# Message sums of a graph network: fp32 products with one-hot matrices widened by ScalarE, in place of three bf16 products with pieces split off by VectorE

## The reference, cut to what matters

```python
def _gnn_layer(nf, traj, src, dst, We, be, Wn, bn):
    ef = jnp.concatenate([nf[src], nf[dst], traj[:, None]], axis=-1)
    msg = jax.nn.leaky_relu(ef @ We.T + be, negative_slope=0.01)
    red = jax.ops.segment_sum(msg, dst, num_segments=nf.shape[0])
    h = jnp.concatenate([nf, red], axis=-1)
    return jax.nn.leaky_relu(h @ Wn.T + bn, negative_slope=0.01)
```

## Time and profile before

| what | value |
|---|---|
| median of runs | 13957.37 us |
| profiled execution | 13966.42 us, span 13965.2 us |
| VectorE (DVE) busy | 10842.4 us, 78% |
| TensorE (PE) busy | 9172.6 us, 66% |
| ScalarE (ACT) busy | 5627.0 us, 40% |
| GpSimd (POOL) busy | 4548.9 us, 33% |
| target phases of the layers | about 7061 to 8575, 9693 to 11210 and 12326 to 13850 us |
| target phase of the first stage | about 4590 to 5955 us |

### The profile page before, as it was taken

One profiled execution on the slowest core, in us unless ns is written; L12 is line 12 of the kernel. 1 busy time (PEld: TensorE's weight loads), 2 busy tenths in 40 slices (PEclk: granted clock), 3 DMA queues, 4 the chain that ended last, 5 costly groups with the idle time before them and its releaser, 6 DMA issues. The chain is left out here.

```text
span 13965.2 us, 514377 instructions
## 1 busy us (share of the span) xinstructions
PE 9172.6 (66%) x172644; PEld 7604.8 (54%) x172644; DVE 10842.4 (78%) x26542; ACT 5627.0 (40%) x15578; POOL 4548.9 (33%) x4413
## 2 busy tenths in 40 slices
PE   6777777762777666667766556666555566666566
PEld 4555555541666555556655554555555555555554
DVE  8999999964777899854479996445999854479997
ACT  4666666630333688743322222333222233322222
POOL 0000000047000677610056663001666600046664
PEclk9999999965555788768899998999999989999997
DMA  1000000011788666746655555666555646665555
GB/s 34 5 5 6 5 5 6 3 25 30 238 241 241 181 197 196 172 129 207 207 180 172 172 171 98 201 201 195 171 171 171 161 123 201 201 188 171 172 172 111
DMA packets 1700459, 1931.56 MB, mean 138 GB/s; under 512 B 222450, under 2 KB 1571268, under 8 KB 1699460
## 3 DMA queue, kind: packets, MB, share of 16 engines
q1 hardware_dynamic: 977585, 893.89, 22.1%
q0 software_dynamic: 199680, 520.06, 15.1%
q10 hardware_dynamic: 522544, 510.34, 10.4%
HBM read 1202.74 MB, written 725.45 MB: 138 GB/s over the span
## 5 line engine op out<-in xcount | busy, mean ns | idle before, releaser
L1563 POOL DMA_INDIRECT work<-rows,quad_at x2928 | 3091.0, 1056 | 4501.8 <-DMA rows<-work 2007.4
L1378 DVE COPY work<-bank 128x256 f32<-128x256 f32 (+1 forms) x3840 | 1630.7, 425 | 1773.0 <-PE bank L1355 1748.6
L1408 PE MATMUL bank<-work 128*128 128x64 bf16 x46848 | 2077.6, 199 | 1361.4 <-DVE hr L1655 1352.2
L1355 PE MATMUL bank<-work 128*128 128x64 bf16 x46080 | 2726.2, 211 | 0.0
L1408 PEld LDWEIGHTS bank<-work 128*128 128x128 fp8e4 (+1 forms) x46848 | 1848.9, 102 | 1517.7 <-issue 1464.9
L1329 ACT COPY work<-tabs 128x192 bf16 x3840 | 1348.9, 351 | 2819.9 <-PE bank L1355 1579.4
L1588 ACT COPY work<-tabs 128x192 bf16 x2928 | 1028.9, 351 | 3548.4 <-PE bank L1604 3242.2
L1355 PEld LDWEIGHTS bank<-work 128*128 128x128 fp8e4 x46080 | 2394.1, 109 | 0.0
L1350 PE MATMUL bank<-wtraj,side 128*128 128x64 bf16 x11520 | 1772.3, 205 | 925.1 <-ACT work L1329 657.8
L521 ACT ACTIVATE work<-work,tabs 128x128 bf16<-128x128 bf16 x6250 | 1919.2, 427 | 935.0 <-DVE work L721 935.0
L1350 PEld LDWEIGHTS bank<-wtraj,side 128*128 128x128 bf16 x11520 | 1194.0, 104 | 1237.4 <-DVE work L1378 580.1
(11 more groups left out here) (323 smaller groups left out, 12309.8 us busy)
## 6 DMA issues: line engine op xcount, KB each, us to landing
work<-hits_g SPq DMA_DIRECT2D x1464, 256.0 KB, 2.7
rows<-work ACTq DMA_DIRECT2D x1440, 256.0 KB, 2.1
work<-hits_s SPq DMA_DIRECT2D x1440, 128.0 KB
hits_g<-work SPq DMA_DIRECT2D x976, 128.0 KB
rows<-work ACTq DMA_DIRECT2D x480, 260.0 KB, 4.6
work<-rows,quad_at POOLq DMA_INDIRECT x3904
work<-meta_src SPq DMA_DIRECT2D x480, 128.0 KB
hits_s<-work SPq DMA_DIRECT2D x480, 128.0 KB, 4.2
```

The source lines that it names most:

```text
L1355: last = ten.matmul(home, hits[n][:, q % GROUP_LOT, slots], window[q % 4][:, k * D:(k + 1) * D], start=False, stop=k == 2, skip_group_chec ...
L1378: vec.tensor_copy(made[n][:, q % GROUP_LOT, :], bank[q % 4][:, 0:QUAD * width]).then_inc(s_read, 1)
L1408: last = ten.matmul(to[:, 0:D], hits_of(j), piece_of(j), start=j == 0 and k == 0, stop=j == QUAD - 1 and k == 2, skip_group_check=True)
L1563: pool.indirect_dma_start(quads[g // 2 % (GATHERED // 2)][:, half(g)], None, table, bass.IndirectOffsetOnAxis(ap=quad_at[:, g:g + 1], axis ...
```

## The change: what it does

In `target_phase`, `less` and `split` go. The message stays one fp32 tile. ScalarE gets a new step, `as_float`: it widens the straight half of a group's one-hots from fp8 to fp32 (128 x 512) into one of four tiles `hits_f`. `scatter` then makes four fp32 products per group in place of twelve bf16 ones. VectorE's order becomes add(p), keep, keep, leaky(p). The semaphores `s_rest` and `s_split` go, and `s_hits` comes. `first_target_phase` now writes the straight one-hots in plain slot order, so its ScalarE cast reads with a stride of two elements; before, the read and the write both ran straight and the two slots of a couple lay interleaved.

```diff
@@ first_target_phase
-                sca.copy(hits_home[q % 4].bitcast(FP8)[:, SLOTS:2 * SLOTS], hits_b[q % 4].rearrange("p j c i -> p (j c i)"),
-                         saturate=False)
+                to = hits_home[q % 4].bitcast(FP8)[:, SLOTS:2 * SLOTS].rearrange("p (j i c) -> p j i c", i=2, c=P)
+                sca.copy(to, hits_b[q % 4].rearrange("p j c i -> p j i c"), saturate=False)
@@ target_phase, tiles
-        msg, rest = ([room.cut(2 * QUAD * D) for _ in range(4)] for _ in range(2))
-        low = [room.cut(QUAD * D, BF16) for _ in range(4)]
+        msg = [room.cut(2 * QUAD * D) for _ in range(4)]
+        hits_f = [room.cut(SLOTS) for _ in range(4)]
@@ scalar
+            def as_float(g, q, lap):
+                sca.wait_ge(s_in[q // 2], since_in + 16 * (lap + 1))
+                at_least(sca, s_sum, g - 3, since)
+                settle(sca, "scalar", g)
+                sca.copy(hits_f[q % 4], hits_home[q // 2][:, q % 2, :].bitcast(FP8)[:, SLOTS:2 * SLOTS]).then_inc(s_hits, 1)
...
                 sca.copy(window[q % 4].unsqueeze(1), tabs[:, 1, bass.ds(w, 1), :]).then_inc(s_window, 1)
+                if not isinstance(g, int) or g >= 2:
+                    as_float(g - 2, (q - 2) % LAP, lap - (q < 2))
@@ tensor, scatter
-                    ten.wait_ge(s_split, since_pairs + lap * (LAP // 2) + (q // 2 + 1))
+                    ten.wait_ge(s_leaky, since_pairs + lap * (LAP // 2) + (q // 2 + 1))
+                ten.wait_ge(s_hits, since + g + 1)
                 at_least(ten, s_kept, g - 3, since)
-                settle(ten, "tensor", g)
...
-                scatter_pieces(ten, sums[q % 4], lambda j: in_twos[:, j // 2, :, j % 2],
-                               [each(upper(msg[q // 2])), each(upper(rest[q // 2])), each(low[q // 2])]).then_inc(s_sum, 1)
+                rows = msg[q // 2][:, half(q)]
+                for j in range(QUAD):
+                    last = ten.matmul(sums[q % 4][:, 0:D], hits_f[q % 4][:, j * P:(j + 1) * P], rows[:, j * D:(j + 1) * D],
+                                      start=j == 0, stop=j == QUAD - 1)
+                last.then_inc(s_sum, 1)
@@ vector
-            def less(p):
...
-            def split(p):
...
-                if 1 <= p <= pairs:
-                    less(p - 1)
-                if p < pairs:
-                    leaky(p)
-                if 1 <= p <= pairs:
-                    split(p - 1)
                 if p >= 3:
                     keep(2 * p - 6)
                     keep(2 * p - 5)
+                if p < pairs:
+                    leaky(p)
```

More of the change, by code:

```diff
@@ L1538, in target_phase @@
         s_in = [sem_of(f"sums_in{n}", True) for n in range(4)]
-        s_window, s_before, s_added, s_leaky, s_rest, s_split, s_sum, s_kept = (sem_of("sums_" + what, True) for what in (
-            "window", "before", "added", "leaky", "rest", "split", "sum", "kept"))
+        s_window, s_before, s_added, s_leaky, s_hits, s_sum, s_kept = (sem_of("sums_" + what, True) for what in (
+            "window", "before", "added", "leaky", "hits", "sum", "kept"))
         past = number - 1
@@ L1588, in step @@
                 sca.copy(window[q % 4].unsqueeze(1), tabs[:, 1, bass.ds(w, 1), :]).then_inc(s_window, 1)
+                if not isinstance(g, int) or g >= 2:
+                    as_float(g - 2, (q - 2) % LAP, lap - (q < 2))
             laps(sca, NG, step)
+            for g in (NG - 2, NG - 1):
+                as_float(g, g % LAP, g // LAP)
         @block.tensor
@@ L1609, in scatter @@
                 if q % 2 == 0:
-                    ten.wait_ge(s_split, since_pairs + lap * (LAP // 2) + (q // 2 + 1))
+                    ten.wait_ge(s_leaky, since_pairs + lap * (LAP // 2) + (q // 2 + 1))
+                ten.wait_ge(s_hits, since + g + 1)
                 at_least(ten, s_kept, g - 3, since)
-                settle(ten, "tensor", g)
-                hits = hits_home[q // 2][:, q % 2, :].bitcast(FP8)
-                each = lambda ap: lambda j: ap[:, half(q)][:, j * D:(j + 1) * D]
-                in_twos = hits[:, SLOTS:2 * SLOTS].rearrange("p (j c i) -> p j c i", c=P, i=2)
-                scatter_pieces(ten, sums[q % 4], lambda j: in_twos[:, j // 2, :, j % 2],
-                               [each(upper(msg[q // 2])), each(upper(rest[q // 2])), each(low[q // 2])]).then_inc(s_sum, 1)
+                rows = msg[q // 2][:, half(q)]
[3 more added lines that the diff above has]
+                last.then_inc(s_sum, 1)
             def step(g, q, lap):
@@ L1640, in leaky @@
                 vec.scalar_tensor_tensor(msg[p % 4], msg[p % 4], SLOPE, msg[p % 4], ALU.mult, ALU.max).then_inc(s_leaky, 1)
-            def less(p):
-                vec.wait_ge(s_leaky, since_pairs + p + 1)
-                vec.tensor_tensor(rest[p % 4], msg[p % 4], upper(msg[p % 4]), ALU.subtract).then_inc(s_rest, 1)
-            def split(p):
-                vec.wait_ge(s_rest, since_pairs + p + 1)
-                vec.tensor_tensor(low[p % 4], rest[p % 4], upper(rest[p % 4]), ALU.subtract).then_inc(s_split, 1)
             def keep(g):
```

## The result

The change makes the kernel slower by more than a tenth. Its executions took 15560.31 to 16355.92 us, against 13954.09 to 13963.7 before; the ratio is 1.1155, with a 95% interval of 1.1133 to 1.1177. Later executions took 16351.26 (e1) and 16346.46 to 16349.05 us (e14, a ratio of 1.172 [1.1686, 1.1754]).

A forecast was written before the change was run, and what follows sets the result against it. VectorE was taken to bound the middle at 3.057 us a pair, then the one-hot load loop at 2.93. 13966 - 164 (middle) + 47 (phase ends) + 15 (low clock) = 13864, less 9 for the runs' median: 13855 us; range 13600 to 14060.

The forecast's parts named there:

- What bounds the kernel before: Target phases: VectorE paces the middle at 3.06 us a pair; the one-hot load loop paces the end, 3.68 measured.
- ScalarE, first stage, VectorE: VectorE falls to 1.85 us a pair, ScalarE needs at most 2.24; first stage's strided cast costs nothing.
- The window copies queued behind the casts: ScalarE copy needed by a pair's second before_message, queued behind as_float's wait: costed at nothing, a few tenths per pair if uncovered.
- The fp32 record: Scatter on TensorE: the weight load sets the pace, 0.111 us a record at 2.4 GHz, 0.22 at 1.2 GHz.
- Rival 3: Scatter's load and product don't overlap: 0.164 us a record, 3.32 a pair, 14380 us total; chance 0.08.
- The loop of load, before_message and scatter: Target phase middle: scatter frees the one-hot load; 5.80 us for two pairs, 2.93 a pair with added waits, 164 us less.
- At the end of a phase: Last 37 pairs of each target phase: 4.1 us a pair taken, 47 us more over three phases.
- GpSimd's floor: Target phase gathers, 1.055 us each with 0.30 between: at least 2.71 us a pair.
- Rival 2: One-hot load in the middle lands later: at 3.0 us, 3.08 a pair, about 14050 us total; chance 0.14.
- Low clock in the middle: Target phases about 2% of the time at 1.2 GHz, about 4.9 us a pair there; 15 us more taken.
- Theory A1: Forecast of e2: array's idle time behind loads keeps the clock low; doubled columns give 2.4 GHz, 13750 to 14050 us.

The follow-up runs named there:

- e1: The changed kernel run again with no edit: 16351.26 us.
- e14: The changed kernel once more, on a chip of the usual pace: 16346.46 and 16349.05 us.
- e4: Changed kernel with twelve bf16 products per group and VectorE's split back, ScalarE's casts kept: 13990.43 us beside 13953.33 for the kernel before.
- e3: Changed kernel with 160 bf16 products of 384 columns ahead of each layer's target phase, as a warm start: 15717.12 us.
- e6: Kernel of e2, with the one-hot load waiting for before_message and as_float of pair p-4, not its scatter: 13455.34 us, ratio 0.9642 to the kernel before.
- e2: Changed kernel with 128 moving columns instead of 64 in each fp32 product of scatter: 13885.18 us.
- e13: Kernel of e2 with 96 moving columns in place of 128, on a chip of the usual pace: 13896.0 us.
- e8: Changed kernel with 64 in place of 128 stationary columns in each fp32 product, leaving out sums of each window's upper half: 13454.46 us.
- e7: Changed kernel, 64 moving columns kept, with one unread bf16 product of 384 columns ahead of each scatter: 14068.04 us.

## Why the prediction was wrong

**What bounds the kernel before: right.** In the middle it is VectorE. e4 puts VectorE's two operations back and has the old pace, which agrees.

**ScalarE, first stage, VectorE: right, but for one wait.** The cast takes 0.618 us (0.62 was taken), and the cast with the strided read lasts 0.619 us (median) as before. VectorE was to be busy near 0.6 of the time; at 2.4 GHz it was, 601.39 of 1088 us (e3), and 35% at 1.2 GHz. The window copies queued behind the casts, which I had costed at nothing, held TensorE for 33.8 us in 118 of the 368 pairs of that stretch, 0.09 us a pair; with the loop opened (e6) these waits are gone.

**The fp32 record: right at both levels.** 0.111 was predicted at 2.4 GHz and 0.112 measured (e2); 0.22 at 1.2 GHz, and 0.213 measured. That the load sets it is shown by the moving columns, 64 (e3), 96 (e13) or 128 (e2) at the same 0.112, and that it goes with the stationary columns by e8. Rival 3 (load and product one after another) falls with them. The way to 0.22 held some luck: the earlier trace rows show no clock level, and the profile has a granted clock of 1.00 from 30 to 31 us, around that product, so "at the low clock level" was read into them because 0.22 is twice 0.111. In rival 3, half of 0.111 is 0.056 and not 0.053, which moves nothing that was forecast.

**The loop of load, before_message and scatter: right in its pace.** 2.93 us a pair was predicted for the middle at 2.4 GHz. 2.96 is measured with 64 columns (e3) and 2.99 with 128 (e2). TensorE's waits for loads came in 124 of e3's 368 pairs and not all through the phase, 69.8 us, so with the window copies 0.28 us a pair where 0.3 to 0.6 were expected. At the end of a phase 4.1 was taken, 3.85 measured. e6 opens the loop and lands on GpSimd's floor, for which I had 2.71; it is 2.64, since a gather there takes 1.02 instead of 1.055. Rival 2 (a later landing) would have shown as over 3.0 a pair in e2 and e3, and fell; a landing time at 2.4 GHz stands in no view of theirs.

**The clock: wrong, and it decides.** The step that failed is "Low clock in the middle": a pair "would need [...] about 4.9 us" at 1.2 GHz (its sum, 1.3 + 16 x 0.22, gives 4.82, and 4.74 was measured, so the price was near), but for how long I wrote "at most 10 us a phase, 30 in all; I take 15, since TensorE is busier than before". It was the whole of every phase: (4.74 - 2.96) x 430 x 3 = 2300 us where I put 15. That this is the level's price and not something else of the change is shown by e3, in which the same products take 2.96 us a pair at 1.00 and 4.75 (380 us for 80 pairs) at 0.50. I took TensorE's busy share for what holds the clock. The changed kernel refutes that as plainly as can be: busy 1313.00 of 1313 us, at 0.50. In the earlier trace rows the kernel before had 785 of 1313 at 0.99. The Trainium skill, in TensorE: Matmul & The Clock Gate, section What's actually happening, says that the clock follows how busy the engine is; read as busy time in the trace, that rule gives 2.4 GHz here, with 2.96 us a pair, and the trace disagrees, with 0.50 and 4.74. What differs is what fills the time. With more moving columns (e2, e13), a bf16 product beside the fp32 ones (e7) or half the stationary columns (e8), the clock is up, in each of the four ways tried. Theory A1 of e2 fits all four, but no row shows the idle time that it speaks of, so what holds the level down stays open.

Two numbers could have warned. The record at 1.2 GHz makes scatter alone 16 x 0.213 = 3.4 us, and with before_message 4.7, over the 3.06 of before: the low level went from costing nothing to costing 1.7 us a pair, so its share mattered for the first time. And a phase can start low, as these stretches of the kernel before show (columns as above):

```profile
7061.00:7112.00 51.00, 31.58 (x710) 28.84 (x711) 41.08 (x83) 12.30 (x35) 37.82 (x38) 0.80 0.60 180
7061.00:7070.00 9.00, 4.21 (x72) 3.89 (x72) 2.87 (x5) 3.16 (x9) 6.86 (x8) 0.56 0.67 206
```

With 0.56 in its first 9 us and 0.99 behind the first 51, the kernel has to climb out of the low level on its own. The kernel before does, and so does the one of e13; the changed one doesn't. I had priced the low state and then weighted it with the share that another mix of work had. No rival carried it, though its time, 4.9 us in all pairs, was worked out ahead of the rivals: 13966 + 1.84 x 1290 = 16340.

## What to carry to other kernels

When a change replaces many light products with few whose stationary operand is fp32, price the stage at both clock levels, and make "stays at the low level" a rival with its own time; a TensorE that is busy all the time proves nothing about the level, so read the granted clock beside it. Where the load of the stationary operand sets the pace, try more moving columns: here 64 more cost nothing per record (0.112 us with 64 and with 128), and the kernel became 2466 us shorter. And when one bound is taken away, look for the buffer whose release hangs on the slowest reader: here a load was freed by scatter, though scatter no longer read it, and freeing it by its real readers brought another 3% (13889.65 to 13455.34 us).

## What the runs showed of the hardware that I had not expected

- An fp32 product is two records, 0.213 us apart at 1.2 GHz and 0.112 at 2.4 GHz with 128 stationary columns, whether 64, 96 or 128 columns move (at 2.4 GHz in e3, e13 and e2); 0.058 with 64 stationary columns (e8).
- TensorE stood at 1.2 GHz for the whole 1313 us stretch without a microsecond of idle time, and at 2.4 GHz in the same phase with 10% of idle time (e2).
- The same program can hold either level: 2.4 GHz for over a millisecond in e3, then 1.2 GHz to the end of the phase. Its three falls stand right behind pauses of TensorE of 0.97, 1.83 and 2.79 us, but a pause of 1.08 us in e3 and one of 2.61 us in e2 brought none.
- A useless bf16 product of 384 columns per group (e7) took the changed kernel from 16349 (e14) to 14068 us.
